# Ternary weights' signs made inside the first self-attention and parked in DRAM, a feed-forward's last downs carried across batches, and a mask added on the vector engine

## The reference

```python
# L0 attention: causal, 16 heads of 32
scores = where(ki > qi, -inf, q @ k.T * scale);  out = softmax(scores) @ v @ wo.T
# L0 feed-forward: quantised activations, ternary weights
def ternary_matmul(x, w): return x @ sign(w).T            # W_g, W_u: 2048 x 512, W_d: 512 x 2048
out = ternary_matmul(silu(ternary_matmul(xq, W_g)) * ternary_matmul(xq, W_u), W_d)
# L1 cross-attention: 16 query heads of 128, 8 key heads, mask over the 256 keys
scores = where(mask, q @ k.T / sqrt(128), -inf);  attn = nan_to_num(softmax(scores))
# L1 feed-forward: both weights and activations rounded to e4m3
h = square(relu(fp8_matmul(x, w_fc)));  out = fp8_matmul(h, w_proj)
```

## Time and profile before

| | us |
|---|---|
| median of three executions | 2538.05 |
| the profiled execution | 2538.91 |
| its span, first to last instruction | 2537.0 |
| first self-attention, block's start to the end of its work | about 23 to 445 |
| preparation of the signs | 1012.4 to 1065.3 |
| ternary feed-forward | 1065.3 to 1337 |
| second cross-attention, main part | about 1485 to 2282 |
| last feed-forward, main part | 2372 to 2537 |

### The profile page before, as it was taken

The page is one execution under the profiler, slowest core; times in us unless marked ns, Lnnn a source line. Parts: engine busy times, 40 slices in busy tenths (PEclk is TensorE's granted clock), DMA queues, the critical chain, the costliest instruction groups (busy, mean ns, idle before and its releaser), DMA issues. The chain is left out here.

```text
span 2537.0 us, 40781 instructions
## 1 busy us (share of the span) xinstructions
PE 2159.8 (85%) x15664; PEld 1831.0 (72%) x15664; DVE 1568.4 (62%) x3131; ACT 1215.2 (48%) x3223; POOL 762.9 (30%) x820
## 2 busy tenths in 40 slices
PE   5999998388888887499997879999999999966876
PEld 5898897266777766377776778888988988853443
DVE  3555664555656554788875645556666666656777
ACT  3555553366666653444333334445555554423466
POOL 2233332666666652044441111111111112220011
PEclk8999999689999987599998989999999999988999
DMA  3000000200000000711101031224324312101000
GB/s 133 1 2 1 2 1 1 75 5 5 5 5 6 5 1 4 256 65 34 34 18 46 1 133 59 93 84 145 113 84 146 112 68 76 51 1 67 6 29 34
DMA packets 42777, 127.17 MB, mean 50 GB/s; under 512 B 3917, under 2 KB 11086, under 8 KB 37593
## 3 DMA queue, kind: packets, MB, share of 16 engines
q1 hardware_dynamic: 42584, 124.56, 14.0%
HBM read 103.57 MB, written 20.97 MB: 49 GB/s over the span
## 5 line engine op out<-in xcount | busy, mean ns | idle before, releaser
L2003 POOL TENSOR_TENSOR x_probs<-x_probs,x_total 128x512 f32<-128x512 f32 x128 | 133.2, 1041 | 595.5 <-DVE x_total L1973 595.3
L1928 ACT ACTIVATE x_probs<-banks,x_nmax 128x256 f32<-128x256 f32 x256 | 119.0, 469 | 213.9 <-DVE x_nmax L1962 213.9
L133 ACT ACTIVATE x_probsT_hi<-banks 128x512 fp32r<-128x512 f32 x256 | 143.7, 607 | 106.8 <-PE banks L1862 101.2
L519 PE MATMUL banks<-x_probsT_hi,x_V_hi 128*128 128x256 f32 x512 | 160.6, 314 | 38.6 <-DVE x_probsT_lo L139 38.0
L139 DVE TENSOR_TENSOR x_probsT_lo<-banks,x_probsT_hi 128x512 fp32r<-128x512 f32 x256 | 165.1, 675 | 45.8 <-ACT x_probsT_hi L133 45.6
L519 PE MATMUL banks<-x_turned,x_wq_hi 128*128 128x256 f32 x1024 | 186.0, 283 | 8.2 <-DVE x_turned L139 8.2
L925 ACT ACTIVATE x_probs<-banks,x_nmax 128x240 f32<-128x240 f32 x256 | 114.4, 460 | 139.8 <-DVE x_nmax L955 139.8
L817 POOL TENSOR_TENSOR x_probs<-x_probs,x_total 128x960 f32<-128x960 f32 (+1 forms) x128 | 130.4, 1040 | 161.3 <-DVE x_total L967 161.3
L448 ACT ACTIVATE a_probs<-banks,a_nmax 128x128 f32<-128x128 f32 (+1 forms) x256 | 104.1, 419 | 126.9 <-DVE a_nmax L464 126.9
L519 PEld LDWEIGHTS banks<-x_turned,x_wq_hi 128*128 128x128 f32 x1024 | 156.8, 189 | 9.4 <-DVE x_turned L139 9.4
L504 POOL TENSOR_TENSOR a_probs<-a_probs,a_total 128x512 f32<-128x512 f32 x64 | 93.9, 1467 | 229.5 <-DVE a_total L474 229.5
(11 more groups left out here) (455 smaller groups left out, 7245.6 us busy)
## 6 DMA issues: line engine op xcount, KB each, us to landing
x_turned<-x_parked SPq DMA_DIRECT2D x24, 1536.0 KB, 6.8
x_parked<-x_turned SPq DMA_DIRECT2D x8, 1536.0 KB, 5.8
x_raw_q<-in_L_xattn_Wq_dram SPq DMA_DIRECT2D x5, 1024.0 KB, 5.2
x_raw_o<-in_L_xattn_Wo_dram SPq DMA_DIRECT2D x5, 1024.0 KB, 8.2
x_all<-in_x_dram SPq DMA_DIRECT2D x2, 2048.0 KB, 18.7
x_ys<-in_ctx_dram SPq DMA_DIRECT2D x16, 256.0 KB, 2.9
f_raw<-in_L_ffn_W_g_dram SPq DMA_DIRECT2D x4, 1024.0 KB, 7.0
f_raw<-in_L_ffn_W_u_dram SPq DMA_DIRECT2D x4, 1024.0 KB, 5.4
```

What stands on the lines that cost most here:

```text
L133: return eng.activation(out, in_, ACT.Copy, scale=scale)
L519: ins = eng.matmul(out, lhs, rhs, start=start and n == 0, stop=stop and n == len(steps) - 1)
L1928: ins = eng.activation(probs[t][r][:, j, :], g.S[:, 2 * t + r, j * S:(j + 1) * S], ACT.Exp, bias=nmax[:, t, r, j:j + 1], accum_out=total[: ...
L2003: eng.tensor_tensor(probs[t][r][:, :, :], probs[t][r][:, :, :], total[:, t, r, :].unsqueeze(2).to_broadcast([P, 2, S]), ALU.mult).then_inc ...
```

## The change

The signs of the ternary weights are no longer made in a block of their own. The first self-attention takes three pieces of 128 x 1024 in each of its eight batches through four new jobs: sload (SP loads a piece), stake (POOL tests for above zero, DVE makes the sign), sturn (eight transposes into a bank, copied out by ACT) and sstore (SP stores the piece to DRAM). Gate and up are parked in bf16, down in fp32. The batch's list and the banks of its jobs are written out by hand in a new order. The POOL copy of x goes, PE turns x itself; V is 416 columns wide per quarter and no longer 512. The ternary block begins with six loads of parked signs, and PE waits for the first two eighths before up 0 and down 0 and for the rest before up 4 and down 4 of batch 0. In the second cross-attention the mask's matmul goes; DVE adds the mask to the scores and takes the maximum in one fused operation per head, which writes the masked scores to SBUF, and the exponential reads them there. In the last feed-forward the last three downs stand between the next batch's ups, and fin and apply two steps later.

```diff
+class Signs:
+    GATE, UP, DOWN = range(3)
+    PIECES, WIDTH = 8, 2 * D
+    def __init__(self, nc, g, w_gate, w_up, w_down):
+        self.w = (w_gate, w_up, w_down)
+        self.parked = [nc.dram_tensor(f"f0_parked_{n}", [P, self.PIECES, self.WIDTH], F32 if n == self.DOWN else BF16, kind="Internal").ap()
+                       for n in range(3)]
+        self.loaded, self.positive, self.signed = (g.sem("f0_w_" + n) for n in ("loaded", "positive", "signed"))
+        self.copied, self.stored = g.sem("f0_w_copied"), g.sem("f0_w_stored")
...
+    order = [
+        (("score", 0, 0), 0), (("max", 0, 0), 0), (("stake", 0), 0), (("exp", 0, 0), 0), (("rec", 0, 0), 0),
+        (("rec", 3, 1), -1), (("k", 1), 0), (("score", 0, 1), 0), (("sturn", 0), 0), (("max", 0, 1), 0),
+        (("pt", 3, 0), -1), (("exp", 0, 1), 0), (("rec", 0, 1), 0), (("scale", 3, 1), -1), (("av", 2), -1),
+        (("scale", 0, 0), 0), (("sload", 1), 0), (("pt", 3, 2), -1), (("score", 1, 0), 0), (("max", 1, 0), 0),
+        (("pt", 3, 1), -1), (("exp", 1, 0), 0), (("pt", 0, 0), 0), (("q", 1), 0), (("sstore", 0), 0),
...
+        (("sstore", 2), 0), (("av", 1), 0), (("scale", 3, 0), 0)]
+    steps = [((0, *job), shift) for job, shift in order]
+    front = [("sload", 0, 0), ("xt", 0, 0), ("xt", 0, 1), ("k", 0, 0), ("q", 0, 0)]
...
-        xs = sb("xs", [P, QT, D])
...
-        V = pair("V", [P, QT, KD, D])
+        WIDE = 3 * 96 + P
+        V = pair("V", [P, QT, KD, WIDE])
+        sign_raw, sign_of = sb("sign_raw", [P, signs.WIDTH]), sb("sign_of", [P, signs.WIDTH], BF16)
+        sign_turned = sb("sign_turned", [P, signs.WIDTH])
...
+        def sign_piece(b, n):
+            return divmod(3 * b.c + n, signs.PIECES)
...
+                if kind == "sload":
+                    if (count := plan.start("sloaded", b, 16, "sload", *a)) >= 16:
+                        eng.wait_ge(signs.signed, count // 16)
+                    which, piece = sign_piece(b, *a)
+                    eng.dma_start(signs.shaped(which, sign_raw[:, :]), signs.source(which, piece)).then_inc(signs.loaded, 16)
+                if kind == "sstore":
+                    which, piece = sign_piece(b, *a)
+                    eng.wait_ge(signs.copied, plan.done("sturned", b, "sturn", *a))
+                    eng.dma_start(signs.parked[which][:, piece, :], sign_tile(which)).then_inc(signs.stored, 16)
+            plan.walk(eng, do)
...
-                    eng.wait_ge(copied, plan.done("copied", b, "xload"))
+                    if b.c == 0:
+                        eng.wait_ge(x_loaded, 32)
+                    x_tile = g.x[:, b.columns(QT, a[0], D)]
                     for kt in range(KD):
...
+                if kind == "sturn":
+                    which, _ = sign_piece(b, *a)
+                    eng.wait_ge(signs.signed, plan.done("staken", b, "stake", *a))
+                    for n in range(signs.WIDTH // P):
+                        at = signs.column(which, n)
+                        ins = eng.transpose(bank.bitcast(BF16)[:, n * P:(n + 1) * P], sign_of[:, at:at + P], g.ident16[:, :])
...
+                    count = plan.done("sturned", b, "sturn", *a)
+                    eng.wait_ge(full, plan.done("full", b, "sturn", *a))
+                    if count > 1:
+                        eng.wait_ge(signs.stored, 16 * (count - 1))
+                    eng.activation(sign_tile(which), g.R[:, plan.buf("R", b, "sturn", *a), :].bitcast(BF16), ACT.Copy).then_inc(signs.copied, 1)
...
+                if kind == "stake":
+                    eng.wait_ge(signs.positive, plan.done("staken", b, "stake", *a))
+                    eng.scalar_tensor_tensor(sign_of[:, :], sign_raw[:, :], 0.0, sign_of[:, :], ALU.is_lt, ALU.subtract,
+                                             reverse1=True).then_inc(signs.signed, 1)
...
+                if kind == "stake":
+                    n, = a
+                    eng.wait_ge(signs.loaded, 16 * plan.done("staken", b, "stake", n))
+                    if (done := plan.done("full", *((b, "sturn", n - 1) if n else (b.plus(-1), "sturn", 2)))) is not None:
+                        eng.wait_ge(full, done)
+                    eng.tensor_scalar(sign_of[:, :], sign_raw[:, :], 0.0, None, ALU.is_gt).then_inc(signs.positive, 1)
...
-                if kind == "xload":
-                    if b.c == 0:
-                        eng.wait_ge(x_loaded, 32)
-                    if (count := plan.done("full", b.plus(-1), "xt", 1)) is not None:
-                        eng.wait_ge(full, count)
-                    eng.tensor_copy(xs[:, :, :].rearrange("p t d -> p (t d)"),
-                                    g.x[:, b.columns(1, 0, QT * D)]).then_inc(copied, 1)
...
-def prepare_signs(nc, g, w_gate, w_up, w_down, gateT, upT, downT):
...
+        PIECES, BOUNDS = signs.PIECES, (0, 2, 8)
+        BEGINS = {2 * at: i for i, at in enumerate(BOUNDS[:-1])}
+        gateT, upT = sb("gateT", [P, PIECES, KD, 2, P], BF16), sb("upT", [P, PIECES, KD, 2, P], BF16)
...
+            eng.wait_ge(signs.stored, 16 * 3 * PIECES)
+            for i, part in enumerate(slice(*ends) for ends in zip(BOUNDS, BOUNDS[1:])):
+                for n, tile in ((signs.GATE, gateT), (signs.UP, upT)):
+                    eng.dma_start(tile[:, part, :, :, :].rearrange("p c k j n -> p c (k j n)"), signs.parked[n][:, part, :]).then_inc(up_loaded[i], 16)
+                eng.dma_start(downT[:, 2 * part.start:2 * part.stop, :].bitcast(F32).rearrange("p (c j) n -> p c (j n)", j=2),
+                              signs.parked[signs.DOWN][:, part, :]).then_inc(down_loaded[i], 16)
...
+                    if b.c == 0 and m in BEGINS:
+                        eng.wait_ge(up_loaded[BEGINS[m]], 32)
...
+                    if b.c == 0 and m in BEGINS:
+                        eng.wait_ge(down_loaded[BEGINS[m]], 16)
...
-                if (count := plan.done("exp", b.plus(-1), "exp", t, r)) is not None:
-                    eng.wait_ge(exped, count)
+                if (count := plan.done("mask", b.plus(-1), "max", t, r)) is not None:
+                    eng.wait_ge(masked_s, count)
                 for j in range(2):
                     out = g.S[:, 2 * t + r, j * S:(j + 1) * S]
-                    eng.matmul(out, first_row[:, :], masked[:, b.columns(1, 0, S)], start=True, stop=False)
                     steps = [(qh[:, 2 * r + j, t * P:(t + 1) * P], kh[:, r, :])
                              for qh, kh in passes(qT[b.parity], kT[b.parity])]
-                    ins = sum_products(eng, out, steps, start=False)
...
-                    ins = eng.activation(probs[t][r][:, j, :], g.S[:, 2 * t + r, j * S:(j + 1) * S], ACT.Exp,
+                    ins = eng.activation(probs[t][r][:, j, :], probs[t][r][:, j, :], ACT.Exp,
...
-                eng.tensor_reduce(nmax[:, t, r, :], g.S[:, 2 * t + r, :].rearrange("p (j k) -> p j k", j=2), AX.X,
-                                  ALU.max, negate=True).then_inc(maxed, 1)
+                for j in range(2):
+                    ins = eng.tensor_tensor_reduce(probs[t][r][:, j, :], g.S[:, 2 * t + r, j * S:(j + 1) * S], masked[:, b.columns(1, 0, S)],
+                                                   1.0, -3.0e38, ALU.add, ALU.max, top[:, t, r, j:j + 1])
+                ins.then_inc(masked_s, 1)
+                eng.wait_ge(masked_s, plan.done("mask", b, "max", t, r))
+                eng.tensor_scalar(nmax[:, t, r, :], top[:, t, r, :], -1.0, None, ALU.mult).then_inc(maxed, 1)
...
-            if prev and m in (1, 3):
-                jobs.append(("fin", -1, m // 2))
-            if prev and m in (4, 6):
-                jobs.append(("apply", -1, m // 2 - 2))
             if m >= LAG:
                 jobs.append(("down", 0, m - LAG))
-        return jobs + [("down", 0, m) for m in range(HT // 2 - LAG, HT // 2)]
+            elif prev:
+                jobs.append(("down", -1, HT // 2 + m - LAG))
+            if prev and m in (3, 4):
+                jobs.append(("fin", -1, m - 3))
+            if prev and m in (6, 7):
+                jobs.append(("apply", -1, m - 6))
+        return jobs
+
+    tail = [("down", 0, m) for m in range(HT // 2 - LAG, HT // 2)]
+    tail += [("fin", 0, 0), ("fin", 0, 1), ("apply", 0, 0), ("apply", 0, 1)]
 
     plan = Plan(
-        [], [slot(c > 0, c < B - 1) for c in range(B)], [("fin", 0, 0), ("fin", 0, 1), ("apply", 0, 0), ("apply", 0, 1)],
+        [], [slot(c > 0, c < B - 1) for c in range(B)], tail,
         events={"full": {"up": 1}, "relu": {"up": 1}, "square": {"up": 1}, "round": {"up": 1}, "down": {"down": 1},
```

215 lines of the change are left out of this document (85 added, 130 removed).

## The result

Four executions of the changed kernel took 2481.51 to 2483.92 us, median 2482.79; the kernel before, run beside it, had a median of 2538.66. The ratio is 0.978, 95% interval 0.9763 to 0.9797. The forecast was 2468 us with a range from 2448 to 2491: the side and the range held, the gain was 55.9 us where 70 were forecast.

What follows compares the result with a forecast made beforehand. Four limits: PE in the first self-attention and second cross-attention, DVE in the ternary preparation, no single engine in the last feed-forward. Terms -31 + 12 - 22 - 29 = -70 gave 2468 us, range 2448 to 2491.

Steps and rivals of the forecast that it cites:

- A: Ternary block: preparation gone gives -52.9 us, a 20 us stall behind sign loads and 2 for slower clock remain; -31 us.
- the load does not stand behind the signs: Rival, ternary block: the fp8 load is not behind the signs or lands early; -51 us, total 2448, chance 0.08.
- B: First self-attention: sign transposes 12.7 us on a full PE, new gaps 1.5, earlier head -2.3; +12 us.
- the prediction's own signs of being wrong: Among them, for the first self-attention: gaps of PE for signs, where its share was to stay above 97%.
- POOL's test (its copy of 128 x 1024 takes 1.04 us): First self-attention: POOL's above-zero test of a sign piece was priced from its copy, 1.04 us.
- beside PE's work: First self-attention: sign operations of POOL, DVE and ACT, three of each a batch, run alongside PE on engines with free time.
- I take 1.5 us for new gaps: First self-attention: allowance for new PE waits if the written order shields the sign operations; 1.5 us.
- POOL and DVE hold each other up: Rival, first self-attention: 24 sign operations each wait out a POOL scaling, 45 us; total 2513, half seen 2490; chance 0.08.
- C: Second cross-attention: 256 mask matmuls go, -33 us, less 8 of longer waits and 3 for late banks; -22 us.
- I give 3 us for the rounds in which PE comes to a bank that DVE frees late: Second cross-attention: allowance for PE waiting on banks that DVE frees late; 3 us lost.
- D: Last feed-forward: downs among the next batch's ups end the drain at 7 boundaries, 15.3 us a batch; -29 us.
- Slower: Rival, second cross-attention: all added latency reaches PE; with a fused operation of 0.69 us total 2617; chance 0.03.

Runs made afterwards that it cites:

- e3: Changed kernel with the first two fp8 loads issued behind the first part of the parked signs instead of behind all signs and prefetches; 2472.7 us.
- e6: Changed kernel with the first two fp8 loads between the second part of the gate and up signs and that of the down signs; 2464.8 us.
- e4: Changed kernel with the above-zero test of each sign piece on DVE instead of POOL; 2467.7 us.
- e1: Changed kernel with the second cross-attention's mask put back as a matmul, reduction and exponential from PSUM; 2502.4 us.
- e7: Changed kernel with the second cross-attention's fused operation taking a negated minimum, so the small operation behind each pair goes; 2479.5 us.
- e9: Changed kernel with e4, e6 and e7 together, plus the next batch's k ahead of the first av from the second cross-attention's second turn; 2445.9 us.
- e2: Changed kernel with the last feed-forward's three downs back at their own batch's end, fin and apply at their old steps; 2511.9 us.
- e5: Changed kernel with the test on DVE as in e4, while POOL makes an unneeded test of 896 columns in the old place; 2466.6 us.

## Why the prediction was right, and where it was not

**A, -31; measured -33.0.** Right in mechanism and size: DVE's wait for the fp8 data was there, and PE stood 16.7 us behind it where 20 were forecast. DVE's wait was 19.4 us, and e3 and e6 show that it hangs on the fp8 loads' place behind the signs: moved ahead, 14 to 18 us come back. e6, whose fp8 data nobody waits for, has the length that the rival "the load does not stand behind the signs" gave, -51: 277.6 us, where 328.5 - 51 is 277.5. The first parked load is issued at 1034.6, not near 1024, because B was twice as long.

**B, +12; measured +23.5.** By the prediction's own signs of being wrong (PE's share under 97%, gaps of PE for signs) this term was wrong. Three sizes were, and they cancel in part. The step that failed first is "POOL's test (its copy of 128 x 1024 takes 1.04 us)": the test takes 2.78 us. From this followed that "beside PE's work" did not hold: "I take 1.5 us for new gaps" was 19.6, 18.1 too little. The sign work itself cost 18.5 us and not 12.7. And the new list, which I had priced at its head alone (-2.3), gave 14.6, 12.3 more. Without this gain, which I had not worked out, B would have been +36: that it missed by 11.5 only is luck.

The rival "POOL and DVE hold each other up", with a chance of 0.08, gave 2490 for half of its price, 22 us, close to the 19.6. Its mechanism is only part of what happened: a scaling held DVE's new operation in seven of 24 cases, for 1.69 us each, 12 us in all, while the wait for the test, 20.9 us, is in neither the forecast nor the rival. The chance was too small all the same. In the kernel before the operation of the earlier trace rows met a scaling in seven of 16 cases and took 1.76 us in each of them; in the other nine it took 0.51 to 0.55, so the price of a meeting is 1.2 us, more than the comparison with a reduction of 0.68 shows. I read the free time of DVE as room. DVE had room, as e4 shows; what it did not have is a queue in which others could pass.

**C, -22; measured -16.4; e1 gives 14 to 17 for it alone.** The mechanism was right. The steady round came as forecast, 0.73 us shorter, and so did the 8 us of longer waits for turned probabilities; PE's work fell by 31.5 us, forecast 33. What was mis-sized is "I give 3 us for the rounds in which PE comes to a bank that DVE frees late": PE's waits grew by 15.1 us in all, so 7 in place of these 3, and they are of another kind. PE's waits for POOL's scalings grew from 7.8 to 16.6 us, which no term had. The loss lies outside of the steady rounds: in the first turn, where x and the context are turned as well, a round fell only from 25.6 to 25.1 us, and the step into the last turn not at all (24.56 and 24.58 us between SP's loads). e7 shows that the chain's length is the cause of few of the waits, e9 that covering one uncovers the next.

**D, -29; measured -28.8.** Right; 15.40 us a batch for the forecast's 15.3, and e2 takes it back.

The four terms with the -1.3 and -0.1 of the blocks between them make -56.1 us, the difference of the spans. "Slower" did not happen: the fused operation costs the 0.41 us taken, not 0.69.

## What to carry to other kernels

An engine's free share tells whether it has time, not whether an operation can be put there: ask what stands behind the operation in its queue, and take its duration from a row with the same operation and types, since the copy and the test of one shape differ here by 2.7 on the same engine. When two engines pass a job to each other, the one that is released can start at the very moment at which the releasing engine starts its next work (here 0.07 us after it, in seven of eight batches); here both halves on DVE, whose test took 0.68 us where POOL's took 2.78, were 17 to 20 us better. Look at the transfer queue in the same way: a load that waits for a result holds every store behind it. A load that is issued last is late by the bytes ahead of it (DVE waited 19.4 us for it here), so order the first loads of a block by when their reader stands in front of the others.

## What I had not expected of the hardware

POOL's comparison of 128 x 1024 fp32 elements into bf16 took 2.78 us, its copy of as many fp32 elements 1.04, DVE's comparison 0.68. A POOL test of 896 columns took 2.61 us in the mean, and 24 of them cost the block nothing that could be told from its own movement (e5).

The second self-attention has the same 688 matmuls in every kernel of this study, and took from 130.1 to 135.5 us, with 101.7 to 107.6 us of PE busy at a granted clock of 0.87 to 0.91. These are its rows in e5_test_twice and e9_k_first:

```profile
1314.29:1444.38 130.09, 101.78 (x688) 92.22 (x688) 81.12 (x173) 40.73 (x95) 14.00 (x34) 0.89 0.07 23
```

```profile
1295.54:1431.07 135.53, 107.59 (x688) 97.52 (x688) 80.98 (x173) 40.68 (x95) 14.03 (x34) 0.87 0.06 22
```

DVE, ACT and POOL do the same in both; only PE's part is longer. The clock of the whole block, 0.89 and 0.87, holds idle time too. Cut into slices of 1 us, PE's busy time is 18.4 us in slices under 0.75 of full clock in e5 and 30.4 in e9; and busy time times granted clock, added up, is 92.7 and 92.2 us, and 92.2 to 92.8 in the seven kernels that I added up. PE does the same work, a different part of it at the lower level. So in a block in which PE pauses often, 5 us of a difference between two kernels can be its clock and nothing that was edited.
